# Turned roots copied one unit earlier, results added at the end of their step, a bank of its own for tile 6's sum

## Time and profile before

| | us |
|---|---|
| median of 3 runs | 327.64 (325.55 to 330.42) |
| the profiled execution, its own time | 330.88 |
| its span, first to last instruction | 329.1 |
| busy: PE, DVE, POOL, ACT | 295.1, 220.5, 186.6, 173.0 |

### The profile page before, as it was taken

One profiled execution on the slowest core, in us unless ns is written; L12 is line 12 of the kernel. 1 busy time (PEld: TensorE's weight loads), 2 busy tenths in 40 slices (PEclk: granted clock), 3 DMA queues, 4 the chain that ended last, 5 costly groups with the idle time before them and its releaser, 6 DMA issues. The chain is left out here.

```text
span 329.1 us, 8914 instructions
## 1 busy us (share of the span) xinstructions
PE 295.1 (90%) x3684; PEld 226.2 (69%) x3684; DVE 220.5 (67%) x569; ACT 173.0 (53%) x246; POOL 186.6 (57%) x152
## 2 busy tenths in 40 slices
PE   7769983979999989999799989999899978979894
PEld 5545763757687768778487767778587766758683
DVE  3533967596469936793479936694569729976682
ACT  2522541945574539535475538545574526665771
POOL 1211445887386756787077765777286744453542
PEclk9995997899999999999799999999999999999999
DMA  6940008000810063003700062003600052007002
GB/s 164 323 139 2 3 31 293 1 2 6 283 36 3 4 235 120 3 2 101 253 2 3 3 210 81 2 2 73 221 1 2 7 190 97 3 11 279 2 0 64
DMA packets 17353, 26.80 MB, mean 81 GB/s; under 512 B 1312, under 2 KB 11552, under 8 KB 17312
## 3 DMA queue, kind: packets, MB, share of 16 engines
q1 hardware_dynamic: 17312, 26.23, 24.6%
HBM read 24.00 MB, written 2.23 MB: 80 GB/s over the span
## 5 line engine op out<-in xcount | busy, mean ns | idle before, releaser
L1068 POOL TENSOR_TENSOR act_lo<-act_sf,act_hi 128x512 fp32r<-128x512 f32 x112 | 146.6, 1329 | 81.8 <-ACT act_sf L965 81.7
L781 DVE SCALAR_TENSOR_TENSOR act_sf<-h_ps,scale 128x1024 f32<-128x1024 f32 x64 | 77.9, 1219 | 74.3 <-DMA scale<-scratch 38.2
L958 ACT ACTIVATE act_hi<-act_sf 128x1024 fp32r<-128x1024 f32 x64 | 68.0, 1063 | 77.7 <-DVE act_sf L781 77.6
L965 ACT ACTIVATE act_sf<-act_sf 128x1024 f32<-128x1024 f32 x64 | 67.3, 1051 | 0.0
L339 PE MATMUL h_ps<-x_hi,w_lo 128*128 128x512 f32 x128 | 57.2, 447 | 4.7 <-DVE act_sf L781 4.7
L354 PE MATMUL y_ps<-act_hi,w_lo 128*128 128x512 f32 x128 | 53.6, 418 | 1.6 <-ACT y_t L975 1.6
L341 PE MATMUL h_ps<-x_hi,w_hi 128*128 128x512 f32 x128 | 51.0, 398 | 0.0
L340 PE MATMUL h_ps<-x_lo,w_hi 128*128 128x512 f32 x128 | 50.9, 398 | 0.0
L355 PE MATMUL y_ps<-act_hi,w_hi 128*128 128x512 f32 x128 | 50.3, 393 | 0.0
L360 PE MATMUL y_ps<-act_lo,w_hi 128*128 128x512 f32 x128 | 40.2, 394 | 0.0
L339 PEld LDWEIGHTS h_ps<-x_hi,w_lo 128*128 128x128 f32 x128 | 24.6, 192 | 12.9 <-DVE act_sf L781 4.9
(11 more groups left out here) (127 smaller groups left out, 392.0 us busy)
## 6 DMA issues: line engine op xcount, KB each, us to landing
scale<-scratch SPq DMA_DIRECT2D x32, 512.0 KB, 5.8
x_t_in<-x_tr SPq DMA_DIRECT2D x8, 256.0 KB, 6.3
x_all<-x SPq DMA_DIRECT2D x8, 256.0 KB, 5.7
out<-out_sb SPq DMA_DIRECT2D x8, 256.0 KB, 2.7
scale<-w SPq DMA_DIRECT2D x1, 1024.0 KB, 7.8
cst<-constants SPq DMA_DIRECT2D x1, 417.0 KB, 5.5
cst<-constants SPq DMA_DIRECT2D x1, 164.0 KB, 5.4
scratch<-combine_t SPq DMA_DIRECT2D x8, 16.0 KB, 1.4
```

Source lines behind the costliest of these rows:

```text
L781: nc.vector.scalar_tensor_tensor(out=act_s[:, u % 2], in0=h_ps[:, u % 2], scalar=0.0, in1=scale[:, f % 2, e].unsqueeze(1).to_broadcast([P, ...
L958: nc.scalar.activation(act_hi[:, u % 4], act_s[:, u % 2], ACT.Square).then_inc(act_hi_ready, 1)
L965: nc.scalar.activation(act_f[:, u % 2], act_s[:, u % 2], ACT.Square).then_inc(act_f_ready, 1)
L1068: nc.gpsimd.tensor_tensor(act_lo[:, u % 4, n], act_f[:, u % 2, n], act_hi[:, u % 4, n].bitcast(F32), ALU.subtract).then_inc(pool_low_ready, 1)
```

## The change

Four things are moved and one bank is exchanged:

- `copy_roots(p)` stands on ACT ahead of `square(u + 6)`, the squares of the seventh expert, in steps 0 to 6; before, behind them.
- `add_experts(f - 1)` stands on DVE at the end of step f; before, it stood behind the first `scale_h` of step f + 1 (and for tile 6 behind the last `low`).
- In step 6 alone, where no attention is left, the router's way is moved: `route(7)` from slot 5 to 4, `shift_logits`, `choose` and `spread_roots` each one unit earlier on DVE, `exponentiate` on ACT and `root_shares` on POOL one unit earlier, and `transpose_roots(7)` from slot 12 to 13, behind the unit's `w2_product`.
- The sum of tile 6 (the seventh) goes into `b2[0]`, bank 2, which is free once tile 7's attention output is copied (`o_t_ready` 8). The first `w2_product` of tile 6 then no longer waits for the copy of tile 5's sum, nor that of tile 7 for the copy of tile 6's.

```diff
+        def sum_bank(f):
+            return b2[0] if f == TILES - 2 else y_ps[:]
...
+                elif e == 0 and f < TILES - 2:
+                    pe.wait_ge(y_t_ready, f)
                 elif e == 0:
-                    pe.wait_ge(y_t_ready, f)
+                    pe.wait_ge(y_t_ready, f - 1)
+                    pe.wait_ge(o_t_ready, TILES)
+                y = sum_bank(f)
...
(the six matmuls of w2_product write y in place of y_ps[:])
...
-                    if n == 5:
+                    if n == (5 if a < TILES else 4):
                         route(p)
-                    if n == 12:
+                    if n == (12 if a < TILES else 13):
                         transpose_roots(p)
...
                 scale_h(f, 0)
                 low(u - 1)
-                if f >= 2:
-                    add_experts(f - 2)
...
                     decay_k(a)
+                if p < TILES <= a:
+                    shift_logits(p)
                 scale_h(f, 3)
                 low(u + 2)
-                if f >= 1 and p < TILES:
+                if f >= 1 and a < TILES:
                     shift_logits(p)
-                if f >= 1 and a < TILES:
                     decay_scores(a, (0, 1))
+                if p < TILES <= a:
+                    choose(p)
                 scale_h(f, 4)
                 low(u + 3)
-                if p < TILES:
+                if a < TILES:
                     choose(p)
-                if a < TILES:
                     decay_scores(a, (2, 3))
+                if p < TILES <= a:
+                    spread_roots(p)
                 scale_h(f, 5)
                 low(u + 4)
-                if p < TILES:
+                if a < TILES:
                     spread_roots(p)
-                if a < TILES:
                     mask_updates(a)
                     scan_states(a)
...
                 low(u + 6)
+                if f >= 1:
+                    add_experts(f - 1)
             low(UNITS - 1)
-            add_experts(TILES - 2)
             add_experts(TILES - 1)
...
-                nc.scalar.copy(y_t[:].rearrange("p g n -> p (g n)"), y_ps[:]).then_inc(y_t_ready, 1)
+                nc.scalar.copy(y_t[:].rearrange("p g n -> p (g n)"), sum_bank(f)).then_inc(y_t_ready, 1)
...
                 square_whole(u + 2)
+                if p < TILES <= a:
+                    exponentiate(p)
                 square(u + 3)
-                if f >= 1 and p < TILES:
+                if f >= 1 and a < TILES:
                     exponentiate(p)
                 square(u + 4)
                 square(u + 5)
-                square(u + 6)
                 if p < TILES:
                     copy_roots(p)
+                square(u + 6)
...
                 low(u + 2)
+                if p < TILES <= a:
+                    root_shares(p)
                 low(u + 3)
-                if p < TILES:
+                if a < TILES:
                     root_shares(p)
```

More of the change, by code:

```diff
@@ L349, in w2_product @@
                     pe.wait_ge(root_t_ready, 1)
+                elif e == 0 and f < TILES - 2:
+                    pe.wait_ge(y_t_ready, f)
                 elif e == 0:
-                    pe.wait_ge(y_t_ready, f)
+                    pe.wait_ge(y_t_ready, f - 1)
+                    pe.wait_ge(o_t_ready, TILES)
+                y = sum_bank(f)
                 pe.wait_ge(act_hi_ready, u + 1)
                 for n in range(HALVES):
-                    pe.matmul(y_ps[:], w2_lo[:, HALVES * e + n], act_hi[:, r, n], start=(e == 0 and n == 0), stop=False)
-                    pe.matmul(y_ps[:], w2_hi[:, HALVES * e + n], act_hi[:, r, n], start=False, stop=False)
+                    pe.matmul(y, w2_lo[:, HALVES * e + n], act_hi[:, r, n], start=(e == 0 and n == 0), stop=False)
+                    pe.matmul(y, w2_hi[:, HALVES * e + n], act_hi[:, r, n], start=False, stop=False)
                 pe.wait_ge(pool_low_ready, pool_lows(u))
@@ L359, in w2_product @@
                 for n in range(HALVES):
-                    last = pe.matmul(y_ps[:], w2_hi[:, HALVES * e + n], act_lo[:, r, n], start=False,
+                    last = pe.matmul(y, w2_hi[:, HALVES * e + n], act_lo[:, r, n], start=False,
                                      stop=(e == EXPERTS - 1 and n == HALVES - 1))
```

## The result

The changed kernel took 310.08 us, median of 4 executions (308.63 to 315.21), against 327.89 for the kernel before (4 executions, 325.55 to 330.42). The ratio is 0.944, interval 0.934 to 0.954, taken over the executions that lie within 1.5% of the fastest of their kernel; between the medians of all four it is 17.8 us faster. The forecast was 314.5 with a range from 310.5, so the direction and the mechanism were right and the time lies 0.4 us under the range. Round by round the difference was 17.8, 15.4 and 12.5 us, with 310.08, 312.20 and 314.69 for the changed kernel, so one median of four to six executions places the gain no better than that.

What follows compares the result with a forecast made beforehand. PE was taken as the bound, by its own work plus its standing; 6.1 + 3.5 + 1.7 + 1.6 + 0.3 + 1.6 = 14.8 us removed gave 316.1 or 312.8, taken as 314.5, range 310.5 to 321.5.

Steps and rivals of the forecast that it cites:

- DVE's 38.2 us: DVE's wait for the broadcast roots before the first scale_h of seven steps; said not to be the price.
- forecast 2.9: Step 4 on ACT: the turned roots stood ready 2.9 us before the input of the seventh expert's squares.
- the 6.1: PE's four waits of project_qk (L393) for the added result, 6.1 us; either move alone would take most.
- Two signs of being wrong: Unit 0 of step 7 still DMA-released with PE standing at L339; ACT idle ahead of L952 in steps 1 to 5.
- 1.7 forecast: Step 3: PE's granted clock at 0.50 for 3.40 us behind a 1.90 us wait; 1.7 us to be regained.
- 1.6 was forecast: First products of tiles 6 and 7 no longer wait for copy_y: 1.6 us in two waits.
- the router's order: Step 6: PE's wait of 1.6 us for combine_r and 0.3 us for copy_roots go.
- DVE did not become the bound: Case 2: DVE sets the last two steps, giving back 4 to 7 us, 318 to 321; chance 0.17.
- The rule of the Trainium skill: Spoke against packing DVE's and POOL's work of step 6 closer; by it the result would be 318 to 321.
- 14.8 us of PE's standing: Sum of all terms, PE's standing or slow time: 6.1 + 3.5 + 1.7 + 1.6 + 0.3 + 1.6 us.
- either 316.0 or 312.8, I take 314.5: End time near 316.0 if the median lacks what is removed, 312.8 (327.6 - 14.8) if not; 314.5 taken.
- extra 3.2 us: The profiled execution of the kernel before lay 3.2 us above the median of the runs (327.64).

Runs made afterwards that it cites:

- add_only: The kernel before with only add_experts moved to the end of its step; 317.27 us, ratio 0.972.
- the two single runs: The kernel before with one move alone: copy_roots ahead of the seventh squares, 314.85 us; or add_experts at the end of its step, 317.27 us.
- no_bank: The changed kernel with the sum of tile 6 back in y_ps and the waits on copy_y back; 314.35 us, ratio 0.960.
- neither: The changed kernel with both moves (copy_roots, add_experts) undone, the bank and step 6's order kept; 324.57 us, ratio 0.986.

## Why the forecast was right in kind and short in size
**The bound.** PE's own standing was the price, not DVE's 38.2 us. Shown by `add_only`: DVE waits on for 30.1 us and the time falls by 9.8.

**The copy and the addition.** Margins and releasers came as worked out: the copy found 2.6 us of cover (forecast 2.9), `scale_h` is released by h, L402 and L499 don't wait in the steps. That either move would take most of the 6.1 by itself is shown by the two single runs; neither has a wait for the added result in its list. Two signs of being wrong showed and cost nothing: unit 0 of step 7 is still released by the broadcast, but PE doesn't stand, and ACT stands 0.3 us ahead of the copy in each of six steps, but the squares' input comes later.

**The clock.** The step with the drop gained 3.83 us. Its gap was 1.90 by the idle column, the rest 1.9, beside 1.7 forecast. From step 1 to the last 2 us no profile of the changed kernel (three) has a drop. The second profile of the kernel before has two, from about 268.5 and 288.9 us, where PE had just stood for 3.0 and 2.1 us; its granted clock in 40 slices:
```profile
PEclk9995995899999999999999999999999998979999
```
The stop of 1.78 us in `no_bank` was followed by one as well, and so was a wait of 1.95 in `add_only`. Waits of 1.4 and 3.1 us in the first profile, of 1.85 in the second, of 2.30 in `neither` and the other stop of 1.78 brought none. So the drops follow PE's standing, but not each time, and the length of the standing alone doesn't say when.

**Step 6 and the bank.** Mis-sized both ways. The bank measured 1.2 where 1.6 was forecast, the router's order 2.4 where 1.9 was (1.6 and 0.3). (A unit's twelve matmuls come to 2.6 us by the row there, not the 2.7 that the forecast put down; nothing hangs on it.) DVE did not become the bound: PE has no gap from 252.0 to 275.5 while DVE is busy for 21.3 of these 23.5 us, as the busy times of this stretch of the changed kernel say:
```profile
252.00:275.50 23.50, 23.50 (x114) 19.31 (x113) 21.32 (x55) 15.79 (x19) 13.34 (x11) 1.00 0.02 5
```
And DVE's timeline of steps 6 and 7:
```profile
268.17 1.31 DVE L770 TENSOR_TENSOR spread<-chosen,root 128x64 f32<-128x64 f32 x1
...
286.26 1.79 DVE L800 TENSOR_TENSOR act_lo<-act_sf,act_hi 128x512 fp32r<-128x512 f32 x1
...
289.12 1.20 DVE L800 TENSOR_TENSOR act_lo<-act_sf,act_hi 128x512 fp32r<-128x512 f32 x1
```
The rule of the Trainium skill that I had set against the change ("SBUF — State Buffer", section "SBUF: two separate sides": such instructions of DVE and GpSimd exclude each other for a whole instruction) is not contradicted: five of the sixteen `low` halves took 1.16 us or more, six in the kernel before, and `spread_roots`' first part 1.31. But DVE had room for them. It decided nothing here.

**The step that failed** is the sum: 14.8 us of PE's standing were too few, and the figure made of it was set too high. The profiles show 16.7 in the first pair and 15.0 in the pair of second ones.

First, the idle column, from which every gap was sized, understates a gap of PE. The ends of matmuls are modelled, and the next matmul can start before that end: in the kernel before, L393 started 1.82 us behind the last L360 in step 5, in the changed kernel 0.23 behind it, a difference of 1.59 where the column said 1.43; the other three boundaries show the same 0.15 or 0.16. If all ten gaps of the sum were short by that much, which is an estimate, it makes some 1.5 us, most of the 1.9 between 14.8 and the 16.7 of the first pair.

Second, "either 316.0 or 312.8, I take 314.5" assumed that the profiled execution's extra 3.2 us might be what the change removes. No run shows where these 3.2 us lay, as the execution at the median has no trace. The one term that could have been missing from the median, the drop of the clock, stood in the second profile of the kernel before as well, twice, in an execution of 328.59. With 16.7 taken from 327.6, the forecast would have been 310.9.

Third, the range's lower end left little room for the start-up's own spread, 7.4 us between two executions of one kernel, in a median of four. That 310.08 was measured is luck in part: over fourteen executions the changed kernel took 313.4, inside the range and nearer to 314.5 than to 310.9, and the change is worth 14.2. Why that is less than the 15.0 to 16.7 of the profiles is not shown. The start-up is one candidate. PE's stops are another: the sum has no term for them, two of them made one of two profiles of the same kernel 3.3 us longer, and three of the ten profiles with an early copy have them, though none of the changed kernel's own three.

## What to carry to other kernels
Price a change by what the bounding engine itself waits for, and look for the one place where its order meets the late chain: here 30 us of another engine's waiting were worth nothing once bank 0 came free in time. Two moves that free the same wait are worth that wait once, so build each alone before adding their gains. Compare start-to-start distances with those of a gapless place to size a gap of PE, and compare stretches rather than whole spans where the start-up varies by more than the effect.

## What the hardware showed that was not expected
The start-up of one unchanged program took 50.2 to 57.6 us to its first `scale_h`; in its three profiles the granted clock was at half for 0, 6.8 and 13.7 us ahead of the first matmul of the experts, and that matmul came the later the longer it had been so. PE stopped for 1.1 to 1.8 us inside a row of small matmuls, in three of the ten profiles with an early copy and in none of the four with a late one (in steps 1 to 7), with no wait in the program; once the clock fell to half behind it, and the step lost 3.6 us where the stop was 1.8. All fourteen profiles have such a stop in the start-up too, of 0.8 to 2.1 us, always ahead of the same matmul, in the changed kernel this one:
```profile
23.09 0.65 PE L480 MATMUL bank<-q_d,state 32*32 32x64 f32 x25 [1.85 <-issue]
```
There as well a packet of 16 KB on the instruction queue landed 1.2 to 1.5 us before PE went on. The traces point to the loading of PE's instructions; what delays it was not settled.
